# Two scaled fp16 parts instead of three bf16 parts in the edge passes of a four-layer graph kernel

## What is computed

```python
# layer 1: hidden row of an edge, summed by target
edge_in = concat([edges, nodes[receivers], nodes[senders]])
h = relu(edge_in @ We1 + be1)
new_edges = h @ We2 + be2
agg = segment_sum(new_edges, receivers)
# layer 2: gated message of an edge, summed by target
k, q, v = x @ W_key + b_key, x @ W_query + b_query, x @ W_value + b_value
gate = sigmoid(k[dst] + q[src])
agg = segment_sum(gate * v[src], dst)
out = agg + x @ W_skip + b_skip
```

## Time and profile before

| what | value |
|---|---|
| median of 3 runs | 4888.29 us (4879.47 to 4893.69) |
| profiled execution, first to last instruction | 4870.2 us |
| total time of the profiled execution beside its span | not given separately |
| mean granted TensorE clock | 0.929 of full |
| busy: TensorE, VectorE, ScalarE, POOL | 4102.1, 3046.8, 1445.4, 2549.3 us |

### The profile page before, as it was taken

One profiled execution on the slowest core, in us unless ns is written; L12 is line 12 of the kernel. 1 busy time (PEld: TensorE's weight loads), 2 busy tenths in 40 slices (PEclk: granted clock), 3 DMA queues, 4 the chain that ended last, 5 costly groups with the idle time before them and its releaser, 6 DMA issues.

```text
span 4870.2 us, 144047 instructions
## 1 busy us (share of the span) xinstructions
PE 4102.1 (84%) x56332; PEld 3693.9 (76%) x56332; DVE 3046.8 (63%) x4215; ACT 1445.4 (30%) x2353; POOL 2549.3 (52%) x2291
## 2 busy tenths in 40 slices
PE   0777799996999983899999998999759999999596
PEld 0666688886999983677777777777559898988496
DVE  5999888882111023677777776777447777777612
ACT  0333499991000003222222222222232222222100
POOL 0388866665656567776666665666003334333200
PEclk9777799998999996999999999999859999999798
DMA  5511388889999974677777776777317666666496
GB/s 170 212 30 30 114 320 324 321 319 306 399 379 418 417 287 165 209 243 235 237 238 239 239 236 220 239 240 240 126 28 247 222 204 220 224 226 204 144 407 257
DMA packets 430171, 1161.15 MB, mean 238 GB/s; under 512 B 111175, under 2 KB 250422, under 8 KB 422712
## 3 DMA queue, kind: packets, MB, share of 16 engines
q1 hardware_dynamic: 331478, 919.45, 53.5%
q0 software_dynamic: 66016, 114.12, 8.1%
q10 hardware_dynamic: 32256, 121.34, 6.4%
HBM read 791.79 MB, written 364.93 MB: 238 GB/s over the span
## 4 chain that ended last, share of the span: by engine, by line
PE 24%; DMA 24%; issue 23%; POOL 12%; DVE 12%; ACT 2%; POOLq 1%; ACTq 1%; SPq 1%; DVEq 0%
DMA feat_slot<-SK,sidx_p 18%; POOL arena L843 6%; POOL feat_slot L920 5%; PE PS L1357 5%; DVE arena L2407 4%; PE PS L1352 4%; PE PS L1363 4%; PE PS L1258 4%; PE PS L1383 2%; ACT arena L1756 2%; DMA sidx_p<-SK 1%; DVE arena L2359 1%; DVE arena L2342 1%; DMA arena<-feat_slot 1%; PE PS L1426 1%
## 5 line engine op out<-in xcount | busy, mean ns | idle before, releaser
L920 POOL DMA_INDIRECT feat_slot<-SK,sidx_p x900 | 1110.8, 1234 | 556.3 <-DMA feat_slot<-SK,sidx_p 283.9
L963 POOL DMA_INDIRECT arena<-tab_l_src,SK x864 | 975.4, 1129 | 470.4 <-DVE arena L2394 226.5
L843 POOL TENSOR_TENSOR arena<-arena 128x448 f32<-128x448 f32 x343 | 365.2, 1065 | 794.5 <-DVE arena L2299 794.5
L1426 PE MATMUL PS<-arena 128*128 128x128 bf16 x7203 | 648.9, 221 | 96.5 <-DVE arena L2342 58.6
L1258 PE MATMUL PS<-arena 128*128 128x192 bf16 (+1 forms) x7203 | 614.5, 248 | 104.7 <-DVE arena L2141 77.7
L1258 PEld LDWEIGHTS PS<-arena 128*128 128x128 bf16 x7203 | 606.0, 98 | 111.8 <-DVE arena L2141 62.1
L1357 PE MATMUL PS<-arena 128*128 (+1 forms) x6267 | 581.2, 221 | 37.0 <-DVE arena L2376 37.0
L1430 PE MATMUL PS<-arena 128*128 (+1 forms) x7203 | 610.5, 194 | 0.9 <-issue 0.9
L2407 DVE TENSOR_TENSOR arena<-arena 128x896 f32<-128x896 f32 (+1 forms) x319 | 329.1, 1032 | 405.3 <-ACT arena L1756 363.6
L1426 PEld LDWEIGHTS PS<-arena 128*128 128x128 bf16 x7203 | 455.7, 98 | 119.5 <-issue 109.6
L1741 ACT ACTIVATE arena<-PS 128x512 f32<-128x512 f32 (+1 forms) x319 | 175.2, 549 | 1091.2 <-PE PS L1363 1073.2
(11 more groups left out here) (254 smaller groups left out, 6683.7 us busy)
## 6 DMA issues: line engine op xcount, KB each, us to landing
arena<-slot_rows SPq DMA_DIRECT2D x343, 448.0 KB
arena<-cnt_t SPq DMA_DIRECT2D x147, 896.0 KB
hots<-arena ACTq DMA_DIRECT2D x175, 672.0 KB
arena<-hots SPq DMA_DIRECT2D x175, 672.0 KB
arena<-cnt_t SPq DMA_DIRECT2D x147, 672.0 KB
cnt_t<-arena SPq DMA_DIRECT2D x49, 1568.0 KB
cnt_s<-arena SPq DMA_DIRECT2D x49, 1568.0 KB
arena<-cnt_s SPq DMA_DIRECT2D x49, 896.0 KB
```

What stands on the lines that cost most here:

```text
L843: pool.tensor_tensor(hid3[i][:, 2 * n:3 * n], hid3[i][:, n:2 * n], upper3[i][:, n:2 * n], ALU.subtract)\
L920: pool.indirect_dma_start(feat_slot, bass.IndirectOffsetOnAxis(ap=sidx_p[odd][:, n:n + 1].bitcast(u32), axis=0), fwin[h][:, t * D:(t + 1) ...
L963: pool.indirect_dma_start(qgot[n % 3][:, slot_of[t] * P:(slot_of[t] + 1) * P], None, tab_src[4], bass.IndirectOffsetOnAxis(ap=gidx[odd][:, ...
L1426: last = nc.tensor.matmul(PS[:, to:to + P], selS[c][:, cut], qsplit[:, (b * 3 + s) * H:(b * 3 + s + 1) * H], start=s == 0, stop=False, ski ...
```

## The change

Tables are multiplied by powers of two, computed on the chip from the norms of the weights (`bound`, `scale_up`, `scale_down`), so that they fit fp16, and split in two fp16 parts. Layer 1's hidden rows keep their three bf16 parts. In layer 2 the messages too become two fp16 parts: ScalarE writes the upper one (`first_half`), VectorE the remainder (`second_half`), and POOL's `last_parts` is gone. The sigmoid and the last addition undo the scale.

```diff
+        wsq = carve(100, 2 * H + 3 * D, parts=D + 1)
+        bound = sb("bound", [P, 3])
+        scale_i = sb("scale_i", [P, 6], i32)
...
-        qsplit = carve(0, NB * 3 * H, bf16)
-        dsplit = carve(36.75, NB * 3 * H, bf16)
+        qsplit = carve(0, NB * 2 * H, f16)
+        dsplit = carve(36.75, NB * 2 * H, f16)
...
-        hid3 = [carve(122.5 + 5.25 * i, 3 * CH * D) for i in range(3)]
+        gated = [carve(122.5 + 3.5 * i, CH * D) for i in range(3)]
+        halves = [carve(124.25 + 3.5 * i, 2 * CH * D, f16) for i in range(3)]
...
-                        pool.wait_ge(msg_res, w * NC + (PLACES + c + 1))
-                        pool.tensor_tensor(hid3[i][:, 2 * n:3 * n], hid3[i][:, n:2 * n], upper3[i][:, n:2 * n], ALU.subtract)\
-                            .then_inc(msg_lo, 1)
...
@@ TensorE, layer 1 and layer 2
-                            for s in range(3):
+                            for s in range(2):
...
-                    parts = upper_[(c + odd) % turns][:, 0:3 * CH * w_].rearrange("p (s j f) -> p s j f", s=3, j=CH)
+                    parts = halves[(c + odd) % turns].rearrange("p (s j f) -> p s j f", s=2, j=CH)
...
@@ ScalarE, slots
-                    with act.Fori(0, NC) as c:
-                        act.wait_ge(splits_res, c + (1 + NC * (2 * m + i)))
-                        nc.scalar.activation(s3[:, bass.ds(c * CH, CH), 1, :], r3[:, bass.ds(c * CH, CH), :], ACT.Copy)\
-                            .then_inc(splits_mid, 1)
...
-                    nc.scalar.activation(hid_[i][:, 0:n].rearrange("p (j f) -> p j f", j=CH), pre3[:, :, 0:D], ACT.Sigmoid)\
-                        .then_inc(gate_made, 1)
+                    nc.scalar.activation(gated[i].rearrange("p (j f) -> p j f", j=CH), pre3[:, :, 0:D], ACT.Sigmoid,
+                                         scale=scale_down[:, 1:2]).then_inc(gate_made, 1)
+
+                def first_half(w, c, odd):
+
+                    i = (c + odd) % turns
+                    act.wait_ge(pre_free, w * NC + (NS * NC + c + 1))
+                    nc.scalar.activation(halves[i][:, 0:CH * w_], gated[i], ACT.Copy).then_inc(msg_hi, 1)
...
                     for c in range(NC):
                         messages(w, c, odd)
+                        if c >= 1:
+                            first_half(w, c - 1, odd)
+                        elif not first:
+                            first_half(w - 1, NC - 1, (odd - 1) % turns)
...
@@ VectorE, fold_weights
+                V.tensor_tensor(wsq[:, 0:2 * H], wpq[:, :], wpq[:, :], ALU.mult)
...
+                step(TS(bound[:, :], bound[:, :], 2.1, 2.0 ** -100, ALU.mult, ALU.max))
...
+                TS(wpq[:, :], wpq[:, :], up[0], None, ALU.mult)
...
@@ VectorE, slots
-                        V.tensor_tensor(r3[:, at, :], t3[:, at, :], s3[:, at, 0, :], ALU.subtract).then_inc(splits_res, 1)
...
-                        V.tensor_tensor(s3[:, at, 2, :], r3[:, at, :], s3[:, at, 1, :], ALU.subtract).then_inc(splits_lo, 1)
+                        V.tensor_tensor(s3[:, at, 1, :], t3[:, at, :], s3[:, at, 0, :], ALU.subtract).then_inc(splits_lo, 1)
...
-                def residual(w, c, odd):
+                def second_half(w, c, odd):
...
-                    dve.wait_ge(pre_free, w * NC + (NS * NC + c + 1))
-                    V.tensor_tensor(hid_[i][:, n:2 * n], hid_[i][:, 0:n], upper_[i][:, 0:n], ALU.subtract).then_inc(msg_res, 1)
+                    dve.wait_ge(msg_hi, w * NC + (c + 1))
+                    V.tensor_tensor(halves[i][:, n:2 * n], gated[i], halves[i][:, 0:n], ALU.subtract).then_inc(msg_lo, 1)
...
-                    V.tensor_tensor(y0[:, w_:2 * w_], y0[:, w_:2 * w_], y0[:, 2 * w_:3 * w_], ALU.add).then_inc(y_step, 1)
```

More of the change, by code:

```diff
@@ L113, in carve @@
             a = int(kb * 256)
-            size = {f32: 4, i32: 4, bf16: 2}[dt] * n
+            size = {f32: 4, i32: 4, bf16: 2, f16: 2}[dt] * n
             b = a + -(-size // 4)
@@ L995, in fold_weights @@
             def fold_weights():
+                pe.wait_ge(fold_kept, 1)
+                nc.tensor.matmul(PS[:, 2048:2048 + 2 * H + 3 * D], wnorm[:, 0:1].to_broadcast((D + 1, P)), wsq[:, :],
+                                 start=True, stop=True).then_inc(fold_made, 1)
                 nc.tensor.transpose(PS[0:D, 0:H], we2[:, :], ident[:, :]).then_inc(fold_made, 1)
-                pe.wait_ge(fold_kept, 1)
+                pe.wait_ge(fold_kept, 2)
                 nc.tensor.matmul(PS[:, 512:512 + H], we2T[:, :], wn1a[:, :], start=True, stop=True)
@@ L1350, in meet @@
                             of = c * CH + b
-                            for s in range(3):
-                                nc.tensor.matmul(PS[:, to:to + P], selp[c % 4][:, cut], qsplit[:, (of * 3 + s) * H:(of * 3 + s + 1) * H],
+                            for s in range(2):
+                                nc.tensor.matmul(PS[:, to:to + P], selp[c % 4][:, cut], qsplit[:, (of * 2 + s) * H:(of * 2 + s + 1) * H],
                                                  start=s == 0 and b < 2, stop=False, skip_group_check=True)
                             cut = slice((CH + b) * P, (CH + b + 1) * P)
-                        for s in range(3):
-                            table = dsplit[:, bass.ds(j * (3 * H) + (s * H + (0 if kind == "slots" else NS * 3 * H)), H)]
+                        for s in range(2):
+                            table = dsplit[:, bass.ds(j * (2 * H) + (s * H + (0 if kind == "slots" else NS * 2 * H)), H)]
                             nc.tensor.matmul(PS[:, to:to + P], (selp[c % 4] if kind == "slots" else seln[c % 3])[:, cut], table,
@@ L1690, in slots @@
                 turns = TURNS[k]
-                hid_, upper_ = (hid, upper) if k == 4 else (hid3, upper3)
                 act.wait_ge(lin_kept_q, UNITS["l1pq"] * (m + 1))
-                for i, (tb, sp_, wd, rest) in enumerate(((NV.rearrange("p b f -> p (b f)"), qsplit, H, qrest), (dtab, dsplit, w_, dtab))):
+                for i, (tb, sp_, wd) in enumerate(((NV.rearrange("p b f -> p (b f)"), qsplit, H), (dtab, dsplit, w_))):
                     if i == 1:
@@ L1696, in slots @@
                     t3 = tb[:, 0:NB * wd].rearrange("p (b f) -> p b f", b=NB)
[L1697 to L1698 removed]
+                    s3 = sp_[:, 0:NB * 2 * wd].rearrange("p (b s f) -> p b s f", b=NB, s=2)
                     with act.Fori(0, NC) as c:
@@ L2254, in slots @@
                 turns = TURNS[k]
-                hid_, upper_ = (hid, upper) if k == 4 else (hid3, upper3)
-                for i, (tb, sp_, wd, rest) in enumerate(((NV.rearrange("p b f -> p (b f)"), qsplit, H, qrest), (dtab, dsplit, w_, dtab))):
+                for i, (tb, sp_, wd) in enumerate(((NV.rearrange("p b f -> p (b f)"), qsplit, H), (dtab, dsplit, w_))):
                     t3 = tb[:, 0:NB * wd].rearrange("p (b f) -> p b f", b=NB)
-                    r3 = rest[:, 0:NB * wd].rearrange("p (b f) -> p b f", b=NB)
-                    s3 = sp_[:, 0:NB * 3 * wd].rearrange("p (b s f) -> p b s f", b=NB, s=3)
+                    s3 = sp_[:, 0:NB * 2 * wd].rearrange("p (b s f) -> p b s f", b=NB, s=2)
                     with dve.Fori(0, NC) as c:
@@ L2520, in _ @@
             fast_or_general(5)
-            step(V.tensor_tensor(XR[:, :, :], XR[:, :, :], sums(D), ALU.add))
+            step(V.scalar_tensor_tensor(XR[:, :, :], sums(D), scale_down[:, 2:3], XR[:, :, :], ALU.mult, ALU.add))
             layer_norm()
```

83 lines of the change are left out of this document (44 added, 39 removed).

## The result

Measured: **4994.58 us** (median of 4 runs, 4985.78 to 4998.53) against 4883.88 us for the kernel before on the same chip (4 runs, 4877.98 to 4893.69). The ratio is 1.0235, 95% interval 1.0208 to 1.0263: slower. The forecast was 4928 us and slower; the measured loss is 111 us where 40 were forecast. The profiled executions differ by nearly the same: spans 4984.2 and 4870.2 us, +114.

What follows compares the result with a forecast made beforehand. It took layer 1 as bound by a ring through TensorE, ScalarE and VectorE's masks, layer 2 by TensorE. Layer 2 +175 and layer 1 -135 made +40 on 4888.29: 4928 us, range 4814 to 5030.

Steps and rivals of the forecast that it cites:

- Sign and mechanism in layer 2: Layer 2's edge pass: VectorE's remainder waits for ScalarE's copy behind the next sigmoid, making the pass slower by 175 us.
- The ring: Layer 2, windows not kept: matmuls, sigmoid, copy, remainder and masks follow without overlap, 3.75 us a chunk, 4.79 at low clock.
- The clock: Layer 2, windows not kept: TensorE's pauses lower the granted clock to 0.72, giving 4.27 us a chunk, 30.3 a window.
- Rival 1: Layer 2: the clock stays up, so the pass costs +61 us and the kernel is faster at 4814 us; chance 0.14.
- rival 2: Layer 2: the clock stays down, so the pass costs +272 us and the kernel takes 5025 us; chance 0.17.
- the term of layer 1: Layer 1's edge pass: each slot chunk saves 0.81 us of table matmuls, natural chunks' saving becomes waiting; -135 us in all.
- Rival 3: Layer 1: POOL's gathers become the bound, so it saves 70 us instead of 135 and the kernel takes 4993; chance 0.10.
- Rival 4: Layer 2: ScalarE's copy comes in time and VectorE bounds windows not kept; pass -169 us, kernel 4584 us; chance 0.04.
- Rival 5: Table matmuls: mixing bf16 masks with fp16 tables costs something, up to the whole saving, kernel over 5025 us; chance 0.03.
- the splitting: Before layer 2's first mask load: fewer conversions and subtractions when splitting the tables, -4 us; in layer 1, 0.

Runs made afterwards that it cites:

- seven buffers: The changed kernel with seven instead of four buffers for the masks and features of layer 1's slot chunks: 4901.19 us, ratio 1.0028 to the kernel before.
- the changed order: The changed kernel with ScalarE's fp16 copy of a chunk's layer 2 messages put ahead of the next chunk's sigmoid: 4680.19 us, ratio 0.9612 to the kernel before.

## Why the prediction was right and wrong

- **Sign and mechanism in layer 2: right.** The ring was there as described, ScalarE's copy always right behind the sigmoid. +193.2 us against +179 with the start of the stage left out. The table matmuls took 2.23 us at the lower level, 2.24 forecast. The ring is 0.1 to 0.15 us longer than its sum for two terms: the way from the last of them to the sigmoid took 0.23 to 0.30, not 0.20, and the sigmoid held ScalarE 0.53 us (4007.96 to 4008.49), not 0.44. I had taken its time from the earlier trace rows, where it has no scale operand: the sigmoid took 0.54 us there, 544 ns in the run without the operand, and 634 ns with it.
- **The clock: right.** I assumed a granted clock of 0.72 in the windows that are not kept, 56% of their time at the lower level; it was 0.72. That this mean of an early stage would hold here was a guess that came true. Windows that are not kept took 28.3 us from first chunk to next window, not 30.3. Kept ones took 17.2 with the loop turns in them, not 14.7: the seventh long step is the one from a kept window's last chunk to the next window's first, and I had counted it on the other side. Two windows together took 45.5 us, 45.0 forecast. (TensorE shows six loop turns in this pass, not the seven that I counted at 4 us each.) TensorE's pauses ahead of chunks with new masks were 1.6 to 2.5 us but for six at loop turns, and its clock fell all the same. Rival 1's sum needs a clock that stays up through such pauses, which no run shows: with like pauses in the kernels without the scale operand and with seven buffers, the granted clock of these windows was 0.73 and 0.70. Rival 1 falls, and so does rival 2.
- **The step that failed: the term of layer 1, "175 slot chunks x 0.81 = 142 us; in the first windows gathers bind, so I take -135 us".** The rows behind it were right for the middle of a pair (8.60 us, forecast 8.58), but I multiplied them over all slot chunks without reading a turn from one pair to the next. There another chain, mask store, reload, transposes, was just hidden and came out: -45.2 us in place of -135, 2.2 us a pair instead of 5.7, and nothing in the last pair and the single window. With seven buffers the middle pairs gave 5.6 us each, which bears out the term for them. The whole pass then is 147.3 us under the kernel before, but that it comes so near the forecast is partly luck: 28 us of it are the end of the pass, where the kernel before too had waited for its buffers. What seven buffers would give the kernel before was not run. The wait was in the trace of before: 19.3 us in 7 waits on the same loads, and I had not asked what ended them.
- **Rival 3** gave 4993 us, the measured time within 2 us, but for another reason. It had layer 1 give half because of POOL's gathers, and the seven buffers show that these keep up. The number is a coincidence: its layer 1 was 25 us too good, and its layer 2 and the time between the passes also differ from what was measured.
- **Rival 4** named 4584 us for a copy that comes in time. In the changed order it comes in time, and layer 2 took 797.5 us with 747 forecast for it. VectorE bounds windows that are not kept with 16.8 us each, 17 forecast; the kept ones took 15.8 with the loop turns in them, not 13.6, again for the long step into the next window.
- **Rival 5** falls: fp16 tables under bf16 masks were taken at the pace of three bf16 parts (a slot chunk's 28 take 1.65 us to the start of the next group, 59 ns each, where the earlier trace rows give 58 for the 42).
- **Between the passes** the change shows -27.7 us, forecast -4. 23 of them are 245 matmuls that the change does not touch and that ran at another clock level: see below. What is left is the 4 that were forecast for the splitting.

## What to carry to other kernels

When a conversion is moved from the engine that made a value to another one, ask what stands ahead of it in that engine's program, and whether that waits for the next step: here the same instructions in the other order are 314 us faster. When a saving per step is multiplied over a loop, read a step where the loop turns as well: here buffers come round after five units there instead of eight, and a store and reload (3.34 and 6.20 us) that was just hidden takes much of the saving back. And an engine freed of work beside a hidden bound shows its worth only when that bound is gone.

## What the runs showed of the hardware

- In a stretch where TensorE computed without a pause the clock still stood at the lower of its two levels, 0.50, for over 50 us. The same 245 matmuls between the passes took 52.5 us at a granted clock of 0.50 in the kernel before and 29.1 at 0.94 in the changed one. 30 us of them in each:

```profile
3573.00:3603.00 30.00, 30.00 (x142) 30.00 (x142) 5.26 (x14) 7.87 (x12) 0.00 (x0) 0.50 0.00 1
```

```profile
3517.00:3547.00 30.00, 29.12 (x245) 28.93 (x245) 9.97 (x28) 13.39 (x19) 0.00 (x0) 0.93 0.00 1
```

  The time between the passes was 172.9 us before and 168.2 and 168.7 with the filled TensorE and the seven buffers, but 145.0 to 146.6 in the other six. In the three long ones the block ran at 0.50, in the six short ones at 0.94 to 0.95, and 23 us of an execution hang on it. Each kernel has one profile, so that the same kernel gets now one level and now the other is not shown, and neither is what decides it; the eight times of the seven-buffer kernel, 4888 to 4912 us with the profiled one at the top, would fit it.
- Twenty small matmuls in each pause brought the granted clock from 0.82 to 0.98, worth 92 us net of their own time.
- With the filling a chunk with new masks took 3.75 us, without it 3.89 at the same level. The 0.14 us lie in two handoffs at TensorE (medians): from the end of the masks to the first table matmul 0.06 instead of 0.13, and from the last group of table matmuls to the sigmoid 0.20 instead of 0.28. Why they are shorter is not shown.
- In the changed kernel the sigmoid with a scale operand for each partition took 634 ns, without it 544, for 448 elements. The copy of 448 elements from SBUF to fp16 took 569 to 577 ns, as its bf16 sister in the earlier trace rows.
- POOL took 1188 ns for the fp16 remainder of 448 elements, VectorE 625. Beside it VectorE's masks took 694 ns instead of 619 and its sum of 64 elements 573 instead of 225.
